# Encoder block with routed experts: the stage behind attention as a list schedule, and the first sequence's out-projection, residual and normalisation inside attention

## The reference

```python
x = x + _L0_attn_ref(_layernorm(x, axis=-1), ...)   # 16 heads of width 8, causal, ALiBi; then out @ Wo + bo
x = x + _L0_ffn_ref(_layernorm(x, axis=-1), ...)    # 8 experts, one per row
x = x + _L1_attn_ref(_layernorm(x, axis=-1), ...)   # attention across the batch of 4
x = x + _L1_ffn_ref(_layernorm(x, axis=-1), ...)
```

```python
logits = x @ Wr + br
probs = jax.nn.softmax(logits, axis=-1)
gate = jnp.max(probs, axis=-1, keepdims=True)
idx = jnp.argmax(probs, axis=-1)
mask = jax.nn.one_hot(idx, E, dtype=jnp.float32)
pos = (jnp.cumsum(mask, axis=0) * mask).astype(jnp.int32)
mask = mask * (pos < C).astype(jnp.float32)
```

## Time and profile before

| | |
|---|---|
| median of 3 runs | 735.17 us (734.15 to 739.01) |
| the profiled execution's own time | 729.13 us |
| its span in the profile | 727.0 us |
| mean granted PE clock | 0.874 of full speed |
| busy: PE, DVE, ACT, POOL | 543.3, 493.9, 440.7, 243.1 us |
| attention's last copy of sums (L833) | 497.1 us |
| first and last row send (L1038) | 552.5 and 592.4 us |
| last row send back (L1044) | about 646 us |

### The profile page before, as it was taken

One profiled execution on the slowest core, in us unless ns is written; L12 is line 12 of the kernel. 1 busy time (PEld: TensorE's weight loads), 2 busy tenths in 40 slices (PEclk: granted clock), 3 DMA queues, 4 the chain that ended last, 5 costly groups with the idle time before them and its releaser, 6 DMA issues. The chain is left out here.

```text
span 727.0 us, 13826 instructions
## 1 busy us (share of the span) xinstructions
PE 543.3 (75%) x4933; PEld 255.0 (35%) x4933; DVE 493.9 (68%) x964; ACT 440.7 (61%) x800; POOL 243.1 (33%) x403
## 2 busy tenths in 40 slices
PE   2775889889988988998898899876777029036774
PEld 1441333232333333333323323213666027024553
DVE  4999779789888988888897888600686306116544
ACT  1970468678877877787787788771244105007773
POOL 2651121221221122122114422210125744758552
PEclk9895699999999999999999999975885559658997
DMA  7488436432304322442432040001112124112012
GB/s 171 109 179 250 112 98 166 100 89 50 83 18 101 81 66 53 108 91 73 96 79 54 6 83 10 9 5 39 45 58 71 54 96 172 32 48 82 16 44 58
DMA packets 64906, 57.30 MB, mean 79 GB/s; under 512 B 12209, under 2 KB 55590, under 8 KB 64828
## 3 DMA queue, kind: packets, MB, share of 16 engines
q1 hardware_dynamic: 56152, 50.15, 27.9%
q10 hardware_dynamic: 6128, 2.90, 1.6%
q0 software_dynamic: 2560, 3.39, 1.4%
HBM read 29.40 MB, written 29.69 MB: 81 GB/s over the span
## 5 line engine op out<-in xcount | busy, mean ns | idle before, releaser
L799 DVE TENSOR_REDUCE neg_max<-bank 128x2 f32<-128x1024 f32 (+2 forms) x320 | 342.9, 1114 | 64.2 <-PE bank L723 62.2
L820 ACT ACTIVATE probs<-ring 128x512 f32<-128x512 f32 (+4 forms) x481 | 302.1, 681 | 83.1 <-PE ring L751 69.9
L751 PE MATMUL ring<-q_operand,k_operand 56*128 56x512 bf16 (+3 forms) x768 | 166.5, 337 | 18.6 <-ACT probs L820 14.5
L772 PE MATMUL sums<-probs,v_all 128*9 128x512 f32 (+3 forms) x1536 | 165.6, 504 | 2.1 <-POOL probs L853 1.5
L853 POOL TENSOR_SCALAR_AFFINE_SELECT probs<-probs 128x512 f32<-128x512 f32 x128 | 80.2, 635 | 220.7 <-ACT probs L820 220.1
L723 PE MATMUL bank<-k_operand,q_operand 54*128 54x512 bf16 (+3 forms) x768 | 145.8, 341 | 7.0 <-DVE v_all L525 5.3
L751 PEld LDWEIGHTS ring<-q_operand,k_operand 56*128 56x128 bf16 x768 | 50.4, 94 | 155.4 <-ACT probs L820 111.0
L717 PE MATMUL bank<-masks 64*128 64x128 bf16 (+2 forms) x768 | 72.5, 225 | 5.3 <-DVE neg_max L799 4.9
L1310 PE MATMUL ring<-sel,ident 128*128 128x256 f32 x50 | 17.4, 525 | 58.6 <-DMA x_rows<-ye,rows 31.1
L723 PEld LDWEIGHTS bank<-k_operand,q_operand 54*128 54x128 bf16 x768 | 46.2, 97 | 24.6 <-DVE neg_max L799 15.1
L717 PEld LDWEIGHTS bank<-masks 64*128 64x128 bf16 x768 | 36.9, 96 | 38.4 <-DVE neg_max L799 25.8
(11 more groups left out here) (154 smaller groups left out, 684.5 us busy)
## 6 DMA issues: line engine op xcount, KB each, us to landing
q_operand<-q_rows SPq DMA_DIRECT2D x64, 96.0 KB, 3.7
k_operand<-k_rows SPq DMA_DIRECT2D x32, 192.0 KB, 4.3
q_rows<-qk_parts SPq DMA_DIRECT2D x36, 128.0 KB, 2.4
k_rows<-qk_parts SPq DMA_DIRECT2D x36, 128.0 KB, 2.4
expert_rows<-fill SPq DMA_DIRECT2D x16, 258.0 KB, 5.1
rows<-expert_rows SPq DMA_DIRECT2D x8, 516.0 KB, 7.0
weighted_sums<-osum SPq DMA_DIRECT2D x128, 18.0 KB
sums_in<-in_L_attn_x SPq DMA_DIRECT2D x4, 512.0 KB, 7.3
```

Of the source, the lines that this page charges most:

```text
L751: last = nc.tensor.matmul(psS[:, bank, w * j:w * j + w], k_op[rows, buf, p, P * kb:P * kb + P], q_op[rows, buf, c, p, q0:q0 + w], start=Tr ...
L772: last = nc.tensor.matmul(psO[32 * i:32 * i + HD + 1, q0:q0 + w], v_all[:, n, kb, i, :], probs[:, u % NPROBS, i // 2, i % 2, 0:w], start=u ...
L799: nc.vector.tensor_reduce(neg_max[:, n % 2, slot, kc, :, pairs[0]:pairs[-1] + 1, t % CH], src, AX.X, ALU.max, negate=True).then_inc(a_read, 1)
L820: nc.scalar.activation(dst, src, ACT.Exp).then_inc(ring_read, 1)
```

## The change

**In attention.** `plan()` gets a fifth kind of item, E, with costs of its own. Sequences 0, 1 and 2 (`EARLY = 3`) have their denominators' reciprocals taken on DVE during the next sequence's groups, stored to DRAM and loaded back broadcast over the rows, and their sums multiplied by them on POOL (two `divide` each). The bias adds move from group 12 on to beside these; those of sequence 3 follow the last one. Sequence 0 goes on, in groups 7 to 11: PE projects its two chunks into a ring bank, ACT copies them to SBUF, POOL adds them to the residual rows, DVE takes the moments, POOL does the power and the scales and normalises its 8 blocks. On SP the 16 filler DMAs follow the operand stores directly, one per A, and the residual loads come at groups 4 to 7. DVE now walks `ORDER` too.

**Behind attention.** All engines walk `ROUTE_ORDER`, made by `route_plan()`, a list scheduler over the steps with costs and dependencies, which takes among the steps that can start soon the one with the longest work behind it. Six chunks are left to project (2 to 7), two to divide. Chunks 2 and 3, and 4 and 5, share one power and one set of scales. The projections of chunks 2 to 5 read the divided sums. The counts of earlier sequences come from a running sum (`seen`), so that each count has 8 or 9 products instead of 8 to 32. The 10 products of `idle_work` ahead of this stage are gone; the 6 ahead of the experts stay. Most of this stage's tiles now lie in one buffer, `early`, which the split operands of preparation used first.

```diff
+EARLY = B - 1
+EARLY_AT = {6: ["reciprocals"], 7: ["store_reciprocals"], 9: ["load_reciprocals"], 20: ["divide"], 21: ["divide"],
+            23: ["bias"], 24: ["bias"]}
+FIRST_AT = {28: ("project", 0), 34: ("project", 1), 40: ("moments", 0), 44: ("moments", 1), 50: ("power", 0), 56: ("scales", 0),
+            **{60 + 2 * i: ("normal", i) for i in range(KB)}}
+PROJECT_TIME, COPY_TIME = 1000, 600
+EARLY_TIME = {"moments": ("dve", 1500), "power": ("pool", 1750), "scales": ("pool", 1000), "normal": ("pool", 800),
+              "reciprocals": ("dve", 960), "divide": ("pool", 1250), "bias": ("pool", 1200)}
...
+            b = (n - H // GH - 1) // (H // GH)
+            tick = (n - H // GH - 1) % (H // GH) * NU + u
+            for name in EARLY_AT.get(tick, []) if 0 <= b < EARLY else []:
+                order.append(("E", n, name, b, int(name in EARLY_AT.get(tick - 1, []))))
...
+            name, c = FIRST_AT.get((n - H // GH - 1) * NU + u, (None, 0))
+            if name == "project":
+                turn += 1
+                order.append(("E", n, name, 0, c, (head, held[head], turn)))
+                pe = max(pe, ring_free[head]) + PROJECT_TIME + 2 * DRAIN
+                act = max(act, pe + SEM) + COPY_TIME
...
-                    elif kind == "A" and n >= 5 and args[0] % 8 == 4 and clears:
+                    elif kind == "A" and clears:
                         clear_slots(sp, clears.popleft())
...
-                        if 7 <= n < 7 + B:
-                            load_residuals(sp, n - 7)
+                        if 4 <= n < 4 + B:
+                            load_residuals(sp, n - 4)
...
+                        pe.wait_ge(at_ready, QC * b + c + 1)
+                        for i in range(CH):
+                            last = nc.tensor.matmul(psS[:, bank, P * i:P * i + P], ot[:, b, CW * c + P * i:CW * c + P * i + P],
+                                                    w["wo"][:, :], start=True, stop=True)
+                        last.then_inc(ring_fill, 1)
...
-                for b in range(B - 1):
+                def reciprocals(b):
                     dve.wait_ge(o_in[b], 32)
                     nc.vector.reciprocal(den[:, b, :], den[:, b, :]).then_inc(rden_ready, 1)
...
+                        nc.scalar.copy(r["st"][:, c, :], psS[:, bank, :]).then_inc(ring_read, 1)
...
+                def divide(b, c):
+                    pool.wait_ge(o_in[b], 32)
+                    pool.wait_ge(rdb_in, 16 * (b + 1))
+                    to = slice(CW * c, CW * c + CW)
+                    nc.gpsimd.tensor_tensor(ot[:, b, to], ot[:, b, to], r["rdb"][:, to], ALU.mult).then_inc(at_ready, 1)
...
+                            last = nc.gpsimd.tensor_scalar(r["xn2"][:, c, :], rows[:, c, X1:X1 + D], r["mv2"][:, c, 0:1],
+                                                           r["nt2"][:, 1, c:c + 1], ALU.subtract, ALU.mult)
...
+GROUPS = [(QC * b, QC * b + 1) for b in range(EARLY)] + [(k,) for k in range(QC * EARLY, CHUNKS)]
...
+        for u in range(KB * r, KB * r + KB):
+            items["send", u] = ("pool", 1280, 0, [("gated", r)] if u < TILES - CH else [("gated_last", 0)])
+    for i in [(name, k) for name in ("project", "add", "apply") for k in GROUPS[0]] + [("power", 0), ("scales", 0)]:
+        del items[i]
...
-        for k in range(CHUNKS):
-            power(k)
         pool.wait_ge(slots_clear, 16 * E * CAP // (2 * P))
         pool.wait_ge(tok_ready, 1)
-        for u in range(TILES):
-            send_rows(u)
+        for name, i in ROUTE_ORDER:
+            if name == "power":
+                power(i)
+            elif name == "send":
+                send_rows(i)
...
-        idle_work(psT2[0], 10)
-        pe.wait_ge(rden_ready, B)
```

548 lines of the change are left out of this document (359 added, 189 removed).

## The result

The changed kernel takes 712.59 us (median of 4 runs, 712.25 to 718.98) where the kernel before takes 737.09 (734.15 to 740.22); the ratio is 0.968, with a 95% interval of 0.962 to 0.974. I had forecast 717.3 in 709 to 727. The sign and the large term were right; the term for attention was not, and the sum is closer to the rival "attention absorbs everything" (711.6) than to my own forecast.

The account below looks back on a forecast made before the run. POOL's 32 row sends behind attention were taken as the bound. Attention +7.7 and the stage behind it -25.6 summed to -17.9 us: 711.2 profiled, 717.3 us carried over to the median, range 709 to 727.

Parts of the forecast that it names:

- large term: Stage behind attention: POOL's last row send done earlier relative to attention's end, gain 25.6 us, bounds 23.5 and 28.5.
- the term for attention: Attention: inserted steps on PE, DVE, POOL and SP lengthen it by 7.7 us, bounds 2 and 12.
- attention absorbs everything: Rival, in attention: idle time hides all inserted steps but PE's 2 us, giving 711.6 us; chance 0.12.
- The bound: Behind attention: POOL's 32 back-to-back row sends hold the end; stage length is first send's start plus 40.8 us.
- The stage's front: Behind attention: first send at H + 19.9 (high clock) or H + 23.3 (low), H being PE's start there.
- The last round: End of the send train: rows at H + 57.5, wanted at H + 56.2; slip 1 to 2 us, low clock only.
- a sign of being wrong: Send train behind attention: forecast is wrong if gaps between sends sum to more than 5 us.
- DVE's third: Attention: a third of DVE's 5.9 us of inserted reciprocals and moments is paid, counted as 2.0 us.
- Carrying over the profile's distance: Whole kernel: profiled execution lay 6.0 us below the runs' median, so 711.2 became 717.3 us.
- Insertions cost their full length: Rival, in attention: each inserted step blocks its engine, 25 to 31 us in all, time 735 to 745; chance 0.06.
- Late round rows: Rival, in the stage behind attention: the round rows come late for POOL's sends; chance 0.13.
- The filler burst: Rival, in attention: SP's 16 filler DMAs stall the scores by 5 to 10 us, time 722 to 727; chance 0.05.

Follow-up runs that it names:

- sends_last: Changed kernel with all of POOL's powers put ahead of the 32 row sends; 718.59 us, 0.991 of the kernel before.
- after_again: Changed kernel with no edit, run again for a second profile; 701.10 us.
- after_timed: Changed kernel with no edit, run once more beside the kernel before; 711.00 us, ratio 0.963.
- idle_back: Changed kernel with the 10 matrix products without use put back ahead of the stage behind attention; 715.62 us, ratio 0.971.
- sets A and C: Two of three sets of follow-up runs, each on one chip; kernel before and changed kernel profiled again in both: spans 727.8 / 699.4 and 740.7 / 708.4 us.
- first pair: Original profiles of the kernel before and the changed kernel, no further edit; spans 727.0 / 717.2 us.
- set B: Follow-up runs on one chip: changed kernel with useless products back, planner costs zeroed, or DVE's or POOL's inserted work repeated; 715.62, 717.58, 713.12, 717.59 us.
- pool_double: Changed kernel with POOL's six inserted divides in attention done twice, unknown to the planner; 717.59 us in one run.
- recosted list: Changed kernel with the list scheduler's costs behind attention taken from its trace and gated rows as single items; 704.91 us, ratio 0.955.
- seq0_behind: Changed kernel with sequence 0's projection, residual, moments and normalisation moved from attention into the scheduled stage; 703.16 us, ratio 0.968.

## Why the prediction was right, and where it was not

**The bound** was named rightly. Putting the train's end back by 17.0 us put 17.5 us of time back (`sends_last`).

**The stage's front.** Forecast H + 19.9 at the higher clock and H + 23.3 at the lower. Measured 21.2 with PE's granted clock at 0.50 in the window of the stage's first 10 us (`after_again`), and 19.2 with it at 0.82 (`after_timed`):

```profile
480.00:490.00 10.00, 7.84 (x56) 1.80 (x60) 0.00 (x0) 8.73 (x16) 1.90 (x3) 1.00 0.00 0
490.00:500.00 10.00, 3.52 (x39) 0.65 (x31) 0.00 (x0) 3.22 (x6) 1.90 (x3) 0.79 0.10 19
500.00:510.00 10.00, 9.71 (x45) 9.52 (x45) 4.29 (x19) 1.17 (x2) 0.00 (x0) 0.50 0.50 138
```

```profile
500.00:510.00 10.00, 8.52 (x59) 8.12 (x59) 5.70 (x29) 1.33 (x3) 0.98 (x1) 0.82 0.60 164
```

The columns are those of the earlier trace rows. In the first execution PE's granted clock is 0.50 in 500 to 510, and PE is busy 9.71 of 10 us. My low-clock sum was 2.1 us too long. It had projection 3 ready at H + 9.5; it was ready at H + 8.0, since groups of 8 products start 1.6 to 1.85 us after one another when they stand back to back; the durations that I added up, 1.9 to 2.1, overlap. DVE's chain from there took 11.2 us where I had 11.8. My high-clock sum has a slip: its terms, 1.3 + 1.16 + 2 x 0.6 + 1.06 + 1.16, give H + 5.9 and not H + 6.2, and so a first send at H + 19.6. The first execution above has a granted clock of 0.50 in H to H + 5 and again in H + 5 to H + 10, the second 0.70 and then 1.00, with the same list; what decided between them I can't tell from the rows. In `idle_back` the clock is at 0.50 in the first 5 us, while the products without use run, and at 0.95 in the next 5; but as told above the same rise came without them in three profiles, so it is not shown to be their work, and they cost more than they bring.

**The last round.** I allowed a slip of 1 to 2 us. There was none in the undisturbed profile, and the last send was done at H + 64.1, inside 62.7 to 67.6. Gain 27.1 for a forecast 25.6 (23.5 to 28.5). In the first profile of after, the gaps between sends sum to 6.1, over the 5 that I had named as a sign of being wrong; the last section says what goes with them.

**Attention: the step that failed.** I had PE 2.3 + DVE 2.0 + POOL 3.1 + SP 0.3 = +7.7, between 2 and 12. Measured is -1.5 and -1.6 in sets A and C, outside these bounds, and +4.1 in the first pair. By its parts, from the table in set B:
- Up to group 3, where only SP's order differs: -0.4, -2.7 and -2.8 in the three pairs, where I had +0.3 for SP.
- PE, DVE, POOL and ACT together: +3.8, +4.9 and +3.7 where I had 7.4, on more work than I counted. DVE's third is the part that a run contradicts: 4.5 us more on it cost 0.1. POOL's lot is 18.9 us, not 15.6, by the rows of after: 6 divides, 8 blocks and 2 adds (the three rows below), a power of 1.7 and 0.8 of small ones.

```profile
L1005 POOL TENSOR_TENSOR sums_in<-sums_in,early 128x512 f32<-128x512 f32 x6 | 7.6, 1273 | 0.0
L1045 POOL TENSOR_SCALAR early<-rows,early 128x128 f32<-128x128 f32 x8 | 6.4, 795 | 0.0
...
L1011 POOL TENSOR_TENSOR rows<-rows,early 128x512 f32<-128x512 f32 x2 | 2.4, 1180 | 5.8 <-ACT early L959 5.8
```

- A block of 128x128 with its two per-partition operands took 795 ns where I put 450. So the price was too low and the share charged too high, and they did not cancel: 3.8 to 5.0 for 18.9 of POOL, 5.6 of DVE and 2.3 of PE.
- The last group, from the row at group 14 to H: -3.7 in set A and -2.5 in set C, where I had nothing, and +0.8 in the first pair. The kernel before has this in its windows, where I did not look:

```profile
480.00:490.00 10.00, 6.79 (x38) 1.14 (x38) 0.00 (x0) 7.15 (x12) 1.69 (x3) 0.81 0.01 2
490.00:500.00 10.00, 6.36 (x40) 1.12 (x40) 0.00 (x0) 3.24 (x6) 2.08 (x4) 0.50 0.06 13
```

PE's granted clock there is 0.81, then 0.50; in the changed kernel above (`after_again`) it is 1.00 and 0.79, and PE had been busy 7.68 and 7.66 us of the 10 ahead of these windows, at full clock in both. The changed kernel's first profile, the one with 32.2 us in the table, has 0.56 and 0.59: the new order does not always keep the clock. That the clock makes the difference fits its own rows: a block of weighted sums (8 products of 512 columns) takes 1.89 in that profile and 1.04 in `after_again`. What decides it was not tried.

The first pair's +4.1 is thus -0.4, +3.8 and +0.8. It looks like a confirmation of my 7.7 in part, and is not one. That the measured time fell into 709 to 727 all the same is owed to the width of the range, whose low end is the best stage with 2 us in attention: the gain of attention that was measured is in none of its terms.

**Carrying over the profile's distance.** I added 6.0 because the profiled execution of before lay 6.0 under its median. That distance is no property of the kernel: the profiled execution of after lay 6.4 over its median, and that of before in set A 3.6 over. The stalls told below, which both kernels have, are of this size; that they make it is not shown, since only profiled executions have a trace.

**The rivals.** *Insertions cost their full length*: excluded, but `pool_double` shows that near half the length is real for work on POOL that the planner does not know. *Late round rows*: the train did break, by 5.3 to 6.1 us, but ahead of the fourth power, which waits for chunk 7's moments, and in the executions with stalls only; the recosted list removes most of it. The 0.13 that I gave it, and its place in the high end of the range, were estimates. That late rows come with the lower clock is not shown: `after_again` and `after_timed` both have a granted clock of 0.50 from 520 to 560, and only `after_timed` has the pause, 5.27 us. *The filler burst*: no stall; the profiles with it are 1.8 us ahead in the mean. *Attention absorbs everything*: nearest in time, by another way than it says: DVE's part was absorbed, POOL's was not, and a lead at group 3 and a shorter last group paid for it.

## What to carry to other kernels

When one engine issues a fixed train of transfers, ask what stands ahead of its first one: here powers and their waits did, and of the 29 us by which the first send moved, 19 are the list that puts only 2 of 4 powers first. An inserted instruction has no price of its own: laid out by a planner that knows it, 27 us on three engines cost 4 to 5; unknown to it, the same steps cost 11.6. To price one, measure between two marks around it, and not at the end of the stage, where other differences of 1 to 3 us between executions come in. And feed a list scheduler with durations at the clock that the stage really runs at, and with items as small as what is waited for; that was worth 6 us more, both together.

## What the runs showed of the hardware

**Stalls while POOL issues indirect DMAs.** In 9 of 14 profiles DVE and ACT wait again and again, up to 11.5 us, for products of PE that have long ended; the profile names no releaser. From the first profile of after, in the experts:

```profile
607.92 2.08 PE L1596 MATMUL ring<-w,hid 128*128 128x128 f32 x8 [0.85 <-ACT hid L1718]
...
614.94 0.69 DVE L1456 TENSOR_TENSOR yb<-ring,b2b 128x512 f32<-128x512 f32 x1 [10.87 <-remote]
...
619.19 0.69 ACT L1718 ACTIVATE hid<-bank,b1c 128x512 f32<-128x512 f32 x1 [11.32 <-remote]
```

PE's products end at 610.0; DVE takes them at 614.94, and all of PE, DVE and ACT stand still meanwhile, but POOL issues one DMA every 1.28 us. The kernel before has the same in set C, in its send train:

```profile
552.55 1.22 POOL L1038 DMA_INDIRECT expert_rows<-rows,slot  x1 [0.20 <-issue]
...
571.80 0.22 DVE L1163 TENSOR_TENSOR pos<-sums,hot 128x64 f32<-128x64 f32 x1 [11.32 <-remote]
...
574.84 0.97 POOL L1038 DMA_INDIRECT expert_rows<-rows,slot  x1 [1.89 <-ACT rows L1455]
...
598.69 0.98 POOL L1038 DMA_INDIRECT expert_rows<-rows,slot  x1 [0.30 <-issue]
```

In the 14 profiles DVE and ACT have no such wait of 2 us or more between 75 us and the first indirect DMA, nor behind the last one, and none at all in the four profiles of set A and the first of the kernel before. The waits lengthen each train: the sends 46.1 for 39.9 in the kernel before, 47.2 and 48.0 for 41.9 after, the sends back 45.6 for 39.8 (42.9 in two profiles). That is 8 to 12 us an execution in either kernel, which is near what lies between the medians of the kernel before in sets A and C, 726.0 and 738.1. It is not a matter of the chip: sets A and B ran on the same one, with medians of the kernel before of 726.0 and 739.6; the four profiles of A have no such wait, and the four of B all have them. That the stalls need the indirect DMAs is what their place suggests; what causes them was not tried, and is open.

**The clock of attention's end.** In the last 20 us of attention PE's granted clock falls to 0.50 (its last 10 us) in all five profiles of `before`'s order and of `seq0_behind`; in eight of the nine that have the first sequence inside it does not (0.77 to 0.93 in the last 10 us), and their last group takes 27.0 to 28.2 us instead of 29.9 to 31.4; the ninth has 0.56 and 0.59, and 32.2 us. It is not in any of the prices that I had taken from the middle of attention.
